# A token embedding whose position table is added by an identity matmul in four of eight groups

## The chip, the core and the metric

The kernel runs on one core of a Trainium2 chip. The metric is the device time of one execution in microseconds (us). Beside the time of each run there is one profiled execution, whose trace gives every instruction's start, duration and what it waited for. All times of the trace count from the start of its span.

## What is computed

Four images of 128 channels and 64 x 64 pixels go through a hybrid block. First the pixels are scored by two depthwise convolutions, and patches of 4 x 4 pixels are ordered by score. Then each pixel becomes a token, and this is the part that the change touches:

```python
pe_re = pe[order]
x_re = jnp.take_along_axis(x_adapted.reshape(B, C, L), order..., axis=2)
x1 = x_re.transpose(0, 2, 1) + pe_re
mu = x1.mean(-1, keepdims=True)
var = ((x1 - mu) ** 2).mean(-1, keepdims=True)
x1n = (x1 - mu) * jax.lax.rsqrt(var + 1e-05) * norm_g + norm_b
```

Behind it come a selective scan over the 4096 tokens, attention with four heads, and a mixture of eight experts. `pe` is the position table, 4096 x 128 float32; adding it and normalising a token do not depend on the order, so the kernel does both before it sorts.

## The kernel before

The program loops over the four images (batches). Each pass is seven stages, each a block in which the five engines run their own instruction lists and meet at the end: `score_and_sort`, `project`, `scan`, `unsort`, `qkv`, `attention`, `ffn`. The change is in `score_and_sort` alone. Nothing reorders the work there: on each engine the instructions run in the order in which the Python code issues them, and semaphores tie the engines together.

The end of `score_and_sort` is the token stage. The 4096 pixels of an image are 32 tiles of 128 tokens, in eight groups g of four tiles (512 columns, `CH`).

- **ScalarE** has earlier copied the pixels into `xp` in patch order (`patches`, L472). In the token stage it has the last Gelu (L495), then a Sigmoid of the head's scores (L498, from PSUM bank 6, waits for semaphore `head`), a Sigmoid of the variance over the channels (L500, waits for `pv`), a square root for the normalisation (L502) and half of the tiles' normalisation (L505).
- **TensorE** runs `token_tiles(g)` (L554 to L563): it transposes the group's four tiles of `xp` into one PSUM bank (`token_bank[g]`, L562) and then adds to semaphore `tr`. It does groups 0 to 5, then the head (`over_channels` with `hwin`, L535, which needs `pv`), then groups 6 and 7, which take the banks of groups 0 and 1 again and so wait until these have been read.
- **VectorE** takes each group in turn (L410 to L422). It adds the bank to the position table `pe_t` and writes the tokens `xt` (L418), then takes `bn_stats` of the four tiles (L422). Before group 2 it computes the variance over the channels (L414 to L416, ends in `pv`). After group 7 follow `bn_aggr` (L425), the final scores (L429 to L434), its half of the normalisation (L440), the rank of each patch and the two slices of the permutation matrix `perm` (L451).
- TensorE transposes each slice of `perm` (L577) and gathers the tokens by matmuls with it (L585); ScalarE takes them out of PSUM (L509), which ends the stage.
- **SyncE** loads the position table by 64 DMAs at the start of the stage (L354, semaphore `pe_in`).

The loop of VectorE before is:

```python
for g in range(NT // 4):
    ...
    dve.wait_ge(tr, g + 1)
    dve.tensor_tensor(xt[...], k.bank(token_bank[g]), pe_t[...], ALU.add).then_inc(k.sem("tokens_embedded"), 1)
    dve.wait_ge(k.sem("tokens_embedded"), g + 1)
    for i in range(4 * g, 4 * g + 4):
        dve.bn_stats(st[:, i, :], xt[:, i * 128:(i + 1) * 128]).then_inc(xt_s, 1)
```

Of the kernel before, what the change touches and what calls it, by code (L numbers as in the profile page):

```python
# [6 lines left out]
ALU, ACT, AX = mybir.AluOpType, mybir.ActivationFunctionType, mybir.AxisListType  # L7
# [3 lines left out]
PS = 4  # L11
NP_ = (H // PS) * (W // PS)
TT = NP_ // 128
# [4 lines left out]
CH = 512  # L18
# [277 lines left out]
def score_and_sort(k, b):  # L296
# [8 lines left out]
    feat, sq, xp = k.at(FEAT_AT, L), k.at(SQ_AT, L), k.at(XP_AT, L)  # L305
# [11 lines left out]
    pe_in, stored = k.sem("pe_in"), k.sem("stored")  # L317
# [7 lines left out]
    xt, pe_t = k.at(XT_AT, L), k.at(PE_AT, L)  # L325
    x1v = k.at(X1_AT, L).rearrange("p (s o) -> p o s", o=OFF)
    tr, xt_s, xtr, std, nrm, pmm = (k.sem(n) for n in ("tr_done", "tokens_stats", "var_ready", "std_ready", "norm_done", "perm_mm"))
# [3 lines left out]
    rs, shift = k.at(LN_AT + 256, NT), k.at(LN_AT + 256 + NT, NT)  # L331
    by_act = [i for i in range(NT) if i % 2]
    token_bank = [4, 5, 0, 1, 2, 3, 4, 5]

    def tap(i, g, j):

        return pad[i][:, RG * g + j // 3:RG * g + j // 3 + RG, j % 3:j % 3 + W]

    def pair(i, g):

        return (NG * i + g) % 3

    def group(t, g):
        return t[:, g * RG * W:(g + 1) * RG * W].rearrange("p (h w) -> p h w", w=W)

    with nc.Block() as block:
# [18 lines left out]
        def _(dve):  # L365
# [44 lines left out]
            for g in range(NT // 4):  # L410
                if g == 2:
                    dve.wait_ge(stored, 32)
                    dve.wait_ge(sums, 2)
                    step(dve.tensor_copy(rows[0], k.bank(6)))  # L414
                    step(dve.scalar_tensor_tensor(rows[1], rows[0], -1.0 / C, rows[0], ALU.mult, ALU.mult))
                    dve.tensor_tensor(rows[1], k.bank(7), rows[1], ALU.add).then_inc(pv, 1)  # L416
                dve.wait_ge(tr, g + 1)
                dve.tensor_tensor(xt[:, g * CH:(g + 1) * CH], k.bank(token_bank[g]), pe_t[:, g * CH:(g + 1) * CH], ALU.add)\  # L418
                    .then_inc(k.sem("tokens_embedded"), 1)
                dve.wait_ge(k.sem("tokens_embedded"), g + 1)  # L420
                for i in range(4 * g, 4 * g + 4):
                    dve.bn_stats(st[:, i, :], xt[:, i * 128:(i + 1) * 128]).then_inc(xt_s, 1)  # L422
            dve.wait_ge(xt_s, NT)
# [32 lines left out]
        def _(act):  # L456
# [36 lines left out]
            for g in range(NG):  # L493
                act.wait_ge(taps_s, (NG + g + 1) * (9 - PT))
                act.activation(group(feat, g), group(feat, g), ACT.Gelu, scale=ca, bias=k.cols[:, C_B2:C_B2 + 1]).then_inc(gelu[1], 1)  # L495
            act.wait_ge(head, 1)
            act.wait_ge(stored, 32)
            act.activation(rows[2], k.bank(6), ACT.Sigmoid, bias=k.cols[:, C_HB:C_HB + 1]).then_inc(sigs, 1)  # L498
            act.wait_ge(pv, 1)
            act.activation(rows[3], rows[1], ACT.Sigmoid, scale=10.0 / (C - 1)).then_inc(sigs, 1)  # L500
            act.wait_ge(xtr, 1)
            act.activation(rs, rs, ACT.Sqrt).then_inc(std, 1)  # L502
            act.wait_ge(shift_s, 1)
# [9 lines left out]
        def _(pe):  # L513
# [40 lines left out]
            def token_tiles(g):  # L554
                if g < 6:
                    pe.wait_ge(taps_s, (2 * NG - 2 + g // 2) * (9 - PT))
                else:
                    pe.wait_ge(k.sem("tokens_embedded"), g - 5)
                pe.wait_ge(k.sem("patches_ready"), g + 1)
                for i in range(4):  # L560
                    at = g * CH + 128 * i
                    last = pe.transpose(k.bank(token_bank[g], 128, 128 * i), xp[:, at:at + 128], k.ident[:, :])  # L562
                last.then_inc(tr, 1)  # L563

            for g in range(6):
                token_tiles(g)
            pe.wait_ge(gelu[1], NG)
            pe.wait_ge(pv, 1)
            over_channels(k.bank(6), k.hwin, lambda n: feat[:, n * CH:(n + 1) * CH]).then_inc(head, 1)
            token_tiles(6)  # L570
            token_tiles(7)
            pe.wait_ge(bd_s, 1)
            pe.matmul(k.bank(3, NP_), k.ones[:, :], bd.rearrange("p n q -> p (n q)"), start=True, stop=True).then_inc(bc, 1)
            for t in range(TT):
                pe.wait_ge(pm, t + 1)
                for u in range(TT):
                    last = pe.transpose(k.bank(7, 128, NP_ * u + 128 * t), k.perm[:, t, 128 * u:128 * u + 128], k.ident[:, :])  # L577
            last.then_inc(pt, 1)
            pe.wait_ge(nrm, NT)
            for o in range(0, OFF, 2):  # L580
                if o == OFF - 2:
                    pe.wait_ge(k.sem("permt_ready"), 1)
                for oo in (o, o + 1):
                    for t in range(TT):
                        last = pe.matmul(k.bank(o // 2, NP_, (oo % 2) * NP_), xt[:, (t * OFF + oo) * 128:(t * OFF + oo + 1) * 128],  # L585
                                         k.perm[:, t, :], start=t == 0, stop=t == TT - 1)
# [1423 lines left out]
def program(nc, ins, out):  # L2010
    with ExitStack() as ctx:
        k = Kernel(nc, ctx, ins, out)
        setup(k)
        with nc.Fori(0, B) as b:
            score_and_sort(k, b)
            project(k)
            scan(k)
            unsort(k, b)
            qkv(k)
            attention(k)  # L2020
            ffn(k, b)
        with nc.Block() as block:
            @block.sync
            def _(sp):
                sp.wait_ge(k.sem("stored"), 32)
# [24 lines left out]
```

## Time and profile before

| | us |
|---|---|
| median of 3 runs | 5550.67 |
| lowest and highest | 5549.47, 5551.52 |
| the profiled execution | 5559.32 |
| its span, first to last instruction | 5557.6 |
| TensorE busy (matmul) | 4773.5 |
| VectorE busy | 4864.6 |
| ScalarE busy | 4017.6 |

The span is the stretch from the first to the last instruction of the profiled execution; its own time is 1.7 us longer, and 8.65 us longer than the median. Every duration of an instruction below is of this one execution. The mean granted clock of TensorE is 0.948 of its full speed. Busy times say how much work an engine has, not who waits for it; for that one reads the timeline of a stage: an idle time behind an instruction stands in square brackets with the engine and line that ended it, and an engine whose rows follow on one another without brackets is the one that the others wait for.

### The profile page before, as it was taken

To read this page: it belongs to the slowest core of one execution; us is meant where nothing else is said; L and a number is where in the kernel's file an instruction comes from. 1 tells how busy PE (TensorE), PEld (TensorE's weight loads), DVE (VectorE), ACT (ScalarE), POOL (GpSimd) and SP (SyncE) were. 2 spreads that over 40 slices of the span, in tenths; PEclk is the share of its full clock that TensorE was granted. 3 is DMA by queue.
4 is the path that set the end of the run, shared out by engine and by line. 5 is a ranking of instruction groups with operands and counts; after the bars stand their busy time and mean duration, and the time that the engine had idled before them with its cause. 6 is when DMAs were issued, how large, how long until landed. Compare 5 with 4: busy or idle time off the path is not lost. (4 is left out here: it accounts for less than half of the span.)

```text
span 5557.6 us, 100602 instructions
## 1 busy us (share of the span) xinstructions
PE 4773.5 (86%) x34168; PEld 1985.8 (36%) x34168; DVE 4864.6 (88%) x6244; ACT 4017.6 (72%) x5832; POOL 1610.2 (29%) x790
## 2 busy tenths in 40 slices
PE   5888879998778887999877887899987788789998
PEld 2333333334333333333433333333343333333334
DVE  6799779998789977999868997799986899689998
ACT  4787569994477757999447784799935778479993
POOL 1388700000048860000004885000000588500000
PEclk9899989999899998999988999899998899999998
DMA  1000030000000003000000000300000000030000
GB/s 41 0 1 0 16 66 10 10 6 24 24 0 1 0 16 66 10 10 6 24 24 0 1 0 16 66 10 10 6 23 24 1 1 0 16 66 10 10 6 31
DMA packets 42112, 89.63 MB, mean 16 GB/s; under 512 B 11595, under 2 KB 27798, under 8 KB 38550
## 3 DMA queue, kind: packets, MB, share of 16 engines
q1 hardware_dynamic: 41622, 83.21, 5.6%
q8 instruction: 294, 4.82, 0.4%
q14 instruction: 196, 1.61, 0.1%
HBM read 28.65 MB, written 8.39 MB: 7 GB/s over the span
## 5 line engine op out<-in xcount | busy, mean ns | idle before, releaser
L1576 ACT ACTIVATE arena<-ps 128x1024 f32<-128x1024 f32 x2048 | 1912.6, 1034 | 190.5 <-PE ps L1539 168.8
L1605 DVE TENSOR_TENSOR arena<-arena 128x1024 f32<-128x1024 f32 x1664 | 1899.6, 1216 | 17.8 <-ACT arena L1576 17.6
L1188 DVE TENSOR_TENSOR_SCAN arena<-ps,hlast,arena 128x512 f32<-128x512 f32 x1024 | 1251.5, 1265 | 28.3 <-ACT hlast L1070 13.9
L1133 POOL TENSOR_TENSOR arena<-arena 128x1024 f32<-128x1024 f32 x512 | 1201.6, 2357 | 240.2 <-ACT arena L1049 173.7
L1539 PE MATMUL ps<-arena 128*32 128x512 f16 x16384 | 1091.0, 382 | 111.2 <-issue 81.0
L1522 PE MATMUL ps<-arena 128*32 128x512 f32 x8192 | 1068.4, 600 | 7.3 <-ACT arena L1576 3.6
L955 PE MATMUL ps<-arena,ident 128*128 128x512 f32 x2048 | 964.8, 595 | 0.0
L1067 ACT ACTIVATE ps<-arena,amat 128x512 f32<-128x512 f32 x1024 | 704.5, 688 | 354.4 <-DVE arena L1188 345.4
L1539 PEld LDWEIGHTS ps<-arena 128*32 128x32 f16 x16384 | 464.6, 97 | 965.9 <-issue 667.8
L1911 POOL MEMSET arena<- 128x1024 f32 x4 | 3.8, 952 | 2452.5 <-POOLq L103 2452.5
L1164 DVE TENSOR_TENSOR arena<-arena,ps 128x1024 f32<-128x1024 f32 x416 | 497.4, 1196 | 80.9 <-PE ps L1024 80.9
L955 PEld LDWEIGHTS ps<-arena,ident 128*128 128x128 f32 x2048 | 392.1, 192 | 354.4 <-issue 326.3
L1522 PEld LDWEIGHTS ps<-arena 128*32 128x32 f32 x8192 | 209.8, 109 | 418.6 <-ACT arena L1576 237.5
L1049 ACT ACTIVATE arena<-ps 128x512 f32<-128x512 f32 x512 | 297.8, 582 | 22.6 <-PE ps L961 22.5
L1024 PE MATMUL ps<-arena,sel 128*128 128x512 bf16 x416 | 164.0, 394 | 138.6 <-DVE arena L1164 125.9
L1989 DVE SCALAR_TENSOR_TENSOR arena<-ps,arena 128x128 f32<-128x128 f32 x1024 | 273.7, 343 | 1.7
L961 PE MATMUL ps<-arena,sel 128*128 128x512 bf16 x512 | 201.1, 393 | 81.0 <-ACT arena L1049 77.7
L1851 PE MATMUL ps<-expw,arena 128*128 128x512 f32 x512 | 252.7, 620 | 11.8 <-DVE arena L1958 8.3
L527 PE MATMUL ps<-arena 128*128 128x512 f32 x512 | 232.4, 615 | 20.0 <-DVE arena L382 20.0
L1122 POOL TENSOR_TENSOR arena<-arena 128x1024 f32<-128x1024 f32 x96 | 226.7, 2361 | 8.6 <-ACT arena L1059 8.6
L643 PE MATMUL ps<-arena,ident 128*128 128x512 f32 x448 | 222.7, 610 | 0.0
L1509 PE MATMUL ps<-arena,ones 128*32 128x512 f32 x1536 | 204.1, 603 | 3.5 <-DVE arena L1605 2.1
(283 smaller groups left out, 4518.4 us busy)
## 6 DMA issues: line engine op xcount, KB each, us to landing
arena<-x SPq DMA_DIRECT2D x36, 512.0 KB, 5.2
arena<-arena SPq DMA_DIRECT2D x64, 256.0 KB, 6.0
arena<-arena SPq DMA_DIRECT2D x64, 224.0 KB, 5.8
arena<-arena SPq DMA_DIRECT2D x28, 512.0 KB, 3.7
arena<-pe SPq DMA_DIRECT2D x256, 32.0 KB, 1.8
out<-arena SPq DMA_DIRECT2D x8, 1024.0 KB, 3.9
expw<-L_ffn_expert_w SPq DMA_DIRECT2D x1, 512.0 KB
wqkv<-L_attn_W_qkv SPq DMA_DIRECT2D x1, 192.0 KB
```

The source lines that it names most:

```text
L955: last = pe.matmul(k.bank(Y_BANK + h), k.ident[:, :], halves(hb[s % RING])[:, h, :], start=False, stop=s == DS - 1)
L1049: act.activation(cs[s % 4], k.bank(C_BANK), ACT.Copy).then_inc(cs_s, 1)
L1067: act.activation(da(s, h), halves(dt[q])[:, h, :], ACT.Exp, scale=k.amat[:, h, s:s + 1]).then_inc(da_s, 1)
L1133: pool.tensor_tensor(halves(hb[s % RING]), halves(hb[s % RING]), cs[s % 4].unsqueeze(1).broadcast_to([128, HD, CH]), ALU.mult).then_inc(hc ...
L1164: dve.tensor_tensor(halves(dbx[(q + owned(s)) % 2]), halves(u[q]), k.bank(B_BANK).unsqueeze(1).broadcast_to([128, HD, CH]), ALU.mult).then ...
L1188: dve.tensor_tensor_scan(halves(hb[s % RING])[:, h, :], da(s, h), halves(injected)[:, h, :], k.hlast[:, s, h, :], ALU.mult, ALU.add).then_ ...
L1522: last = pe.matmul(k.ps[32 * h:32 * h + 32, O * CH:(O + 1) * CH], v[:, j * 128 + 32 * h:j * 128 + 32 * h + 32], probs[(2 * j + h // 2) % 8 ...
L1539: last = pe.matmul(k.ps[32 * t:32 * t + 32, (2 * group[p] + e) * CH:(2 * group[p] + e + 1) * CH], ks[:, h, j * 128 + 32 * t:j * 128 + 32 * ...
L1576: act.activation(probs[p % 8], k.bank(2 * group[p], 2 * CH), ACT.Exp, scale=SCALE / SPLIT ** 2).then_inc(exp_s, 1)
L1605: dve.tensor_tensor(acc[p % 2], acc[p % 2], probs[p % 8], ALU.add).then_inc(acc_s, 1)
L1851: pe.matmul(k.bank(expert_bank(i, hb)), tnt[:, i * 128:(i + 1) * 128], k.expw[:, hb * HE:hb * HE + HE, :].rearrange("p e c -> p (e c)"), s ...
L1989: dve.scalar_tensor_tensor(tile, k.bank(expert_bank(i, hb), C, e * C), gate[:, i, hb * HE + e:hb * HE + e + 1], tile, ALU.mult, ALU.add).t ...
```

## The change

The position table is added on another engine for groups 2, 4, 5 and 7. There TensorE first multiplies the identity with the group's 512 columns of `pe_t` into the bank (`start=True`), and then adds the four tiles of `xp` by ordinary accumulating matmuls against the identity, in place of transposes. ScalarE copies the bank to `xt` and adds to a new semaphore `tokens_copied`; VectorE waits for that and only takes the statistics. The other four groups stay as they were. ScalarE's copies of groups 2, 4 and 5 stand behind the last Gelu and ahead of the two Sigmoids, that of group 7 behind them.

```diff
+    added_by_pe = (2, 4, 5, 7)
+    embedded_v, embedded_a = k.sem("tokens_embedded"), k.sem("tokens_copied")
...
+    def wait_embedded(eng, g):
+        by_act_ = g in added_by_pe
+        eng.wait_ge(embedded_a if by_act_ else embedded_v, sum((o in added_by_pe) == by_act_ for o in range(g + 1)))
...
                 dve.wait_ge(tr, g + 1)
-                dve.tensor_tensor(xt[:, g * CH:(g + 1) * CH], k.bank(token_bank[g]), pe_t[:, g * CH:(g + 1) * CH], ALU.add)\
-                    .then_inc(k.sem("tokens_embedded"), 1)
-                dve.wait_ge(k.sem("tokens_embedded"), g + 1)
+                if g not in added_by_pe:
+                    dve.tensor_tensor(xt[:, g * CH:(g + 1) * CH], k.bank(token_bank[g]), pe_t[:, g * CH:(g + 1) * CH], ALU.add)\
+                        .then_inc(embedded_v, 1)
+                wait_embedded(dve, g)
...
+            def copy_tokens(g):
+                act.wait_ge(tr, g + 1)
+                act.activation(xt[:, g * CH:(g + 1) * CH], k.bank(token_bank[g]), ACT.Copy).then_inc(embedded_a, 1)
+
+            for g in added_by_pe:
+                if g < 6:
+                    copy_tokens(g)
             act.wait_ge(head, 1)
...
+            for g in added_by_pe:
+                if g >= 6:
+                    copy_tokens(g)
             act.wait_ge(xtr, 1)
...
                 else:
-                    pe.wait_ge(k.sem("tokens_embedded"), g - 5)
+                    wait_embedded(pe, g - 6)
                 pe.wait_ge(k.sem("patches_ready"), g + 1)
+                if g == 0:
+                    pe.wait_ge(pe_in, 16 * TT * PS * 8)
+                if g in added_by_pe:
+                    pe.matmul(k.bank(token_bank[g]), k.ident[:, :], pe_t[:, g * CH:(g + 1) * CH], start=True, stop=False)
                 for i in range(4):
                     at = g * CH + 128 * i
-                    last = pe.transpose(k.bank(token_bank[g], 128, 128 * i), xp[:, at:at + 128], k.ident[:, :])
+                    out = k.bank(token_bank[g], 128, 128 * i)
+                    if g in added_by_pe:
+                        last = pe.matmul(out, xp[:, at:at + 128], k.ident[:, :], start=False, stop=i == 3)
+                    else:
+                        last = pe.transpose(out, xp[:, at:at + 128], k.ident[:, :])
                 last.then_inc(tr, 1)
```

TensorE's instructions of the token stage, from group 2 to the last group, are these before (groups 2 to 5, the head, groups 6 and 7; L562 is a transpose of one tile):

```order
L562 MATMUL ps<-ident,arena 128x128 [waits patches_ready,taps_added]
L562 MATMUL ps<-ident,arena 128x128 x3
L535 MATMUL ps<-arena,hwin 32x512 [waits pv_ready,gelu2_done]
L535 MATMUL ps<-arena,hwin 32x512 x7
L562 MATMUL ps<-ident,arena 128x128 [waits patches_ready,tokens_embedded]
L562 MATMUL ps<-ident,arena 128x128 x3
L573 MATMUL ps<-arena,ones 128x256 [waits scores_spread]
```

(The first two rows stand there once for each of the groups 0 to 5, the fifth and sixth for each of the groups 6 and 7.) With the change they are:

```order
L581 MATMUL ps<-arena,ident 128x512 [waits patches_ready,taps_added]
L586 MATMUL ps<-ident,arena 128x128 x4
L588 MATMUL ps<-ident,arena 128x128 [waits patches_ready,taps_added]
L588 MATMUL ps<-ident,arena 128x128 x3
L581 MATMUL ps<-arena,ident 128x512 [waits patches_ready,taps_added]
L586 MATMUL ps<-ident,arena 128x128 x4
L581 MATMUL ps<-arena,ident 128x512 [waits patches_ready,taps_added]
L586 MATMUL ps<-ident,arena 128x128 x4
L553 MATMUL ps<-arena,hwin 32x512 [waits pv_ready,gelu2_done]
L553 MATMUL ps<-arena,hwin 32x512 x7
L588 MATMUL ps<-ident,arena 128x128 [waits patches_ready,tokens_embedded]
L588 MATMUL ps<-ident,arena 128x128 x3
L581 MATMUL ps<-arena,ident 128x512 [waits patches_ready,tokens_embedded]
L586 MATMUL ps<-ident,arena 128x128 x4
```

Three of the four added groups stand in front of the head (L553), one behind it; each has the identity matmul (L581) and four accumulating matmuls (L586) where there were four transposes. A float32 matmul that is no transpose is one row here and two instructions in the trace.

ScalarE's instructions between the last Gelu and the square root are these before:

```order
L495 ACTIVATE arena<-arena,cols,small 128x1024 [waits taps_added] x3
L498 ACT_TABLE_LOAD [waits stored]
L498 ACTIVATE arena<-ps,cols 128x512 [waits head_mm]
L500 ACTIVATE arena<-arena 128x512 [waits pv_ready]
L502 ACT_TABLE_LOAD
L502 ACTIVATE arena<-arena 128x32 [waits var_ready]
```

And with the change:

```order
L503 ACTIVATE arena<-arena,cols,small 128x1024 [waits taps_added] x3
L506 ACTIVATE arena<-ps 128x512 [waits tr_done] x3
L513 ACT_TABLE_LOAD [waits stored]
L513 ACTIVATE arena<-ps,cols 128x512 [waits head_mm]
L515 ACTIVATE arena<-arena 128x512 [waits pv_ready]
L506 ACTIVATE arena<-ps 128x512 [waits tr_done]
L520 ACT_TABLE_LOAD
L520 ACTIVATE arena<-arena 128x32 [waits var_ready]
```

The copies (L506) stand around the two Sigmoids, three ahead and one behind, and both table loads stand behind a copy.

On VectorE the add before the statistics is gone in four groups, whose statistics (now L430) wait for `tokens_copied`.

## Rows read from the trace of the kernel before

**Rows 1.** The page's table of busy time by engine.

```profile
PE 4773.5 (86%) x34168; PEld 1985.8 (36%) x34168; DVE 4864.6 (88%) x6244; ACT 4017.6 (72%) x5832; POOL 1610.2 (29%) x790
```

**Rows 2.** Timeline of VectorE, first batch: start, length, engine, line, operation, [idle before].

```profile
106.48 0.69 DVE L418 TENSOR_TENSOR arena<-ps,arena 128x512 f32<-128x512 f32 x1 [3.01 <-PE ps L562]
107.20 0.87 DVE L422 BATCH_NORM_STATS2 arena<-arena 128x6 f32<-128x128 f32 x4
107.99 0.67 DVE L418 TENSOR_TENSOR arena<-ps,arena 128x512 f32<-128x512 f32 x1
...
109.49 0.67 DVE L414 COPY arena<-ps 128x512 f32<-128x512 f32 x1
...
111.53 0.68 DVE L418 TENSOR_TENSOR arena<-ps,arena 128x512 f32<-128x512 f32 x1
112.25 0.87 DVE L422 BATCH_NORM_STATS2 arena<-arena 128x6 f32<-128x128 f32 x4
...
119.74 0.88 DVE L422 BATCH_NORM_STATS2 arena<-arena 128x6 f32<-128x128 f32 x4
```

**Rows 3.** The same timeline at the end of the stage, VectorE and TensorE.

```profile
133.71 0.35 DVE L451 TENSOR_SCALAR perm<-iota,small 128x256 f32<-128x256 bf16 x1
...
134.12 0.69 PE L577 MATMUL ps<-ident,perm 128*128 128x128 f32 x2 [0.96 <-DVE perm L451]
134.60 15.41 PE L585 MATMUL ps<-perm,arena 128*128 128x256 f32 x64
```

**Rows 4.** Timeline of TensorE in the token stage, first batch.

```profile
105.72 2.84 PE L562 MATMUL ps<-ident,arena 128*128 128x128 f32 x24
111.76 1.92 PE L535 MATMUL ps<-arena,hwin 128*32 128x512 f32 x16 [3.21 <-DVE arena L416]
113.62 1.09 PE L562 MATMUL ps<-ident,arena 128*128 128x128 f32 x8
...
125.78 1.22 PE L573 MATMUL ps<-arena,ones 128*128 128x256 f32 x2 [11.07 <-DVE arena L434]
```

**Rows 5.** Timeline of ScalarE in the token stage, first batch.

```profile
104.76 1.28 ACT L498 ACT_TABLE_LOAD   x1
113.74 0.69 ACT L498 ACTIVATE arena<-ps,cols 128x512 f32<-128x512 f32 x1 [7.70 <-PE ps L535]
...
114.97 1.28 ACT L502 ACT_TABLE_LOAD   x1
```

**Rows 6.** Timeline of TensorE in the convolution: float32 matmuls over 512 columns.

```profile
59.56 28.06 PE L527 MATMUL ps<-arena 128*128 128x512 f32 x65
```

**Rows 7.** Timeline of TensorE in the last stage, first batch: float32 matmuls over 128 columns.

```profile
1305.58 1.91 PE L1826 MATMUL ps<-wout,arena 128*128 128x128 f32 x8
...
1309.97 0.38 PE L1822 MATMUL ps<-outb,ones 128*128 128x512 bf16 x1
1310.19 1.05 PE L1826 MATMUL ps<-wout,arena 128*128 128x128 f32 x8
1311.08 0.38 PE L1822 MATMUL ps<-outb,ones 128*128 128x512 bf16 x1
```

**Rows 8.** Timeline of SyncE's queue: the last loads of the position table.

```profile
59.82 7.36 SPq L354 DMA_DIRECT2D arena<-pe  x16
```

**Rows 9.** ScalarE's copies from PSUM in the next stage: duration min/median/max in ns.

```profile
L778 ACT ACTIVATE arena<-ps x64: 575/598/604, 153.3 to 4324.5; 128x512 f32<-128x512 f32 x64
```

**Rows 10.** Stretches: length, busy PE, PEld, DVE, ACT, POOL, granted clock, DMA share, GB/s.

```profile
1491.50:1494.60 3.10, 0.00 (x0) 0.00 (x0) 3.00 (x9) 0.00 (x0) 0.00 (x0) 1.00 0.00 0
1494.60:1497.10 2.50, 2.42 (x17) 0.58 (x18) 2.43 (x9) 0.00 (x0) 0.00 (x0) 0.78 0.04 7
1497.10:1499.00 1.90, 1.89 (x8) 1.49 (x8) 1.87 (x9) 1.85 (x3) 0.00 (x0) 0.50 0.00 0
1305.50:1307.30 1.80, 1.80 (x10) 1.66 (x9) 0.00 (x0) 0.94 (x1) 0.61 (x1) 0.50 0.40 86
```

**Rows 11.** Timeline of TensorE, second batch: the last eight transposes.

```profile
1497.02 1.97 PE L562 MATMUL ps<-ident,arena 128*128 128x128 f32 x8
```

## The prediction, on record before the changed kernel ran

> **What bounds the kernel now.** I read the page's busy table first. VectorE is busy for 88% of the span and TensorE for 86% [rows 1]; such averages over stages do not say who is waited for in the token stage, so I read that stage by its timeline, in the first of the four batches. The chain of waits is of no use here, since it covers only the last per cent of the span.
>
> VectorE's timeline shows no gap from 106.48 us on [rows 2]. Each of the eight groups costs it an add (L418) and four statistics (L422). From one add to its statistics it is 0.72 us (106.48 to 107.20), from the statistics to the next instruction 0.79 us (107.20 to 107.99), so 1.50 us a group; before group 2 it does the variance over the channels, 2.04 us (109.49 to 111.53). The last statistics start at 119.74. From there VectorE goes on without a gap, through the aggregates and the scores, to the second slice of the permutation at 133.71; 0.4 us later TensorE transposes it (134.12), and the gather matmuls follow at once (134.60) [rows 3]. A microsecond that VectorE saves before 119.74 is therefore a microsecond off the stage, and there are four batches.
>
> TensorE has much slack there [rows 4]: six groups of transposes issued by 108.3, nothing until the head's matmuls at 111.76 (they wait for VectorE's L416), the last two groups from 113.62, and the next matmul of all at 125.78. ScalarE has more [rows 5]: it loads the Sigmoid table at 104.76, waits until 113.74, runs two Sigmoids and loads the Sqrt table at 114.97, which is used only behind VectorE's last statistics.
>
> About 0.2% of this kernel, 11.1 us, is what a measurement can tell from no change; that is 2.8 us a batch.
>
> **The change, part by part.**
> 1. *Four adds leave VectorE* (groups 2, 4, 5, 7): 4 x 0.71 to 0.72 = 2.85 us a batch, 11.4 us in all. This is the ceiling of the gain: nothing else is taken away.
>
> 2. *TensorE gets work.* No row shows an identity matmul in this place, but its two forms stand elsewhere. A float32 matmul over 512 columns is two instructions in the trace; 65 of them take 28.06 us, so 0.86 us for one matmul [rows 6]. Four float32 matmuls over 128 columns are eight instructions; they and one bf16 matmul over 512 columns repeat every 1.11 us (1309.97 to 1311.08), of which the bf16 one takes 0.22 (1309.97 to 1310.19), leaving 0.89 us [rows 7]. An added group is thus 0.86 + 0.89 = 1.75 us. The transposes that it replaces take 0.11 each (24 in 2.84), 0.43 a group [rows 4]. For a bound below, 1.3 us (0.86 for the table and transposes' own price for the rest); above, 0.86 + 4 x 0.43 = 2.6 us, were each small matmul four transposes long. I take 1.75, the row of the same form.
>    The Trainium skill ("TensorE: Matmul & The Clock Gate", Terms) speaks against this edit: transpose mode is four times faster for FP32. By it the added group is the 2.6 us; by the rows the ratio is two (0.22 to 0.11).
>
> 3. *Where that puts TensorE.* From 105.72: groups 0 and 1 0.87, group 2 1.75, group 3 0.43, groups 4 and 5 3.50: issued by 112.27. Only then comes the head, which was ready from 111.7: 1.86 (111.76 to 113.62), so 114.13. Group 6 is issued by 114.56, group 7 by 116.31; with 0.16 for the tail of the last matmul (0.27 long, 0.11 apart), 116.47. The work that is moved in front of the head costs the head 0.5 us, which nobody waits for, as VectorE wants the Sigmoids only behind group 7's statistics. The new wait for the position table at group 0 costs nothing: its loads are issued by 67.2 [rows 8], and VectorE waited for them before, at the same place.
>
> 4. *ScalarE gets four copies* out of PSUM, 0.60 each, by the row of the same shape [rows 9]. From a result of TensorE to its reader I take 0.17 us: group 0's transposes end at about 106.31, the add starts at 106.48. Copies 2 and 4 end near 109.3 and 111.5. Copy 5 starts at 112.60 (112.27 + 0.16 + 0.17), ends at 113.20. The Sigmoid table load now stands behind it: 113.20 to 114.48, and the head's result is there at 114.4, so Sigmoids to about 115.7 (1.23 for both, 113.74 to 114.97 [rows 5]). Copy 7 is ready at 116.64 and finds ScalarE free by 0.9 us; it ends at 117.24. The Sqrt table load then ends at 118.5, while VectorE still aggregates. The order of instructions shows no table load between Gelu and Copy.
>    The Trainium skill ("ScalarE: Activation LUTs", What ACT_TABLE_LOAD costs) puts a load at about 2.7 us with its drain, where this trace has 1.28. By the page ScalarE would be free for copy 7 only at 117.1, the statistics would start at 117.8, and the sum below would be 7.8 us instead of 9.8.
>
> 5. *VectorE waits for copies.* Without waits its statistics would start at 111.53, 113.02, 113.81, 114.60, 116.10 and 116.89 for groups 2 to 7 (112.25 and 1.50 more for each further group, less 0.71 to 0.72 for each add taken out). Copies 2, 4 and 5 are there at 109.3, 111.5 and 113.3, so 1.3 us or more early; group 6's tokens at 114.9, wanted at 115.39. Only group 7 is late: copy 7 ends at 117.24, plus 0.06, so 117.30. VectorE waits 0.41 us, and behind that wait stand the aggregates and all that follows.
>
> 6. *Sum.* 119.74 - 117.30 = 2.44 us a batch, 2.85 less a wait of 0.41; four batches 9.8 us. The profiled execution, 5559.32 us (span 5557.6), would become 5549.5. The median of the runs, 5550.67, lies 8.65 below the profiled one; I take the same 9.8 off it: 5540.9. In the other three batches the same rows stand with the same distances, save that in the second TensorE's clock was at half for the end of the stretch (below); it makes no difference before.
>
> Twenty-four more TensorE instructions a batch, 96 in all, must be fetched; I cost that at nothing beside the 34168 that it has [rows 1].
>
> **The rivals.**
> - *No wait at all.* If the added group costs 1.6 us or less, or results are seen sooner, copy 7 is there by 116.89, and the whole 2.85 comes: 5539.3, 0.205% faster. 0.4 us of TensorE is only 4% of 10.6, which speaks for it; that both prices are of the same form speaks against. The latencies were also taken generously. Chance 0.16.
> - *ScalarE late.* If the load behind copy 5 held it for twice its row, 2.57 us, copy 7 would start at 117.0: 5542.5. The load's row is 1.28 in every place, against it. Chance 0.08.
> - *A small float32 matmul costs four transposes* (the mechanism of the page in part 2). 0.84 more a group, 3.36 in all: group 7's statistics start at 120.66, 0.92 later than before; 5554.3, slower by 0.07%. Rows 7 speak against it directly. Chance 0.06.
> - *TensorE becomes the bound, at half clock* (the rival on the slower side). TensorE may be 2.44 us later than in part 3 before the gain is gone, and 5.2 us before the kernel is slower by over 0.2%. In the second batch the granted clock fell from 1.00 to 0.78 in the head's stretch and to 0.50 behind it, after 3.1 us without a matmul [rows 10]; eight transposes then took 1.97 us instead of 1.09 [rows 11], and eight float32 matmuls at 0.50 1.91 instead of 1.05 [rows 7]. If it is at half from 111.5, the last 4.8 us take 4.8 more, and the statistics start at 122.1: 9.4 us slower in all, 5560; if for the whole stretch, 10.6 more: about 5583. Against it: the pause after which it fell is filled by the change, and until the pause is over the clock stands at 1.00, the higher level of 2.4 GHz [rows 10]. If half clock comes in one batch only, 4.8 of the 9.8 us are lost. Chance 0.05.
> - *Nothing moves*, because what follows is set by something that I don't see (the gather's start, or TensorE's clock at the gather): 5550.7. VectorE's unbroken row of work speaks against it. Chance 0.05.
>
> The forecast has the remaining 0.60, with 5539 to 5544 for itself.
>
> **How the numbers follow.** The range takes the forecast, the first two rivals and a part of the losses in between (one batch at half clock, 5545.7), with a microsecond or two below the ceiling's 5539.3, as much as the runs shown spread (5549.47 to 5551.52): 5537.5 to 5548.0; left out are the last three, 0.16. Faster by over 0.2% (below 5539.6) is the first rival and a little of the forecast's edge: 0.18. Slower by over 0.2% (above 5561.8) is the half clock: 0.05. Within: 0.77.
>
> **What would show it.** In the changed profile: L426 has 16 instructions instead of 32; TensorE's added group is 1.75 us long and its clock 1.00 between 105 and 116; the copies take 0.60; the statistics of group 7 start at 117.3 with an idle of about 0.4 ended by ScalarE, and nothing else on VectorE waits; the gather starts at 132.2. Wrong it is if VectorE also waits at groups 4 to 6, if a wait on TensorE's side is longer than 2.4 us, or if the 2.4 us are there at the aggregates and gone at the gather.

## The result and the profile after

The change makes the kernel slower: 5583.99 us median (5575.99 to 5587.52) against 5551.52 (5549.47 to 5561.6) for the kernel before beside it. The ratio is 1.005, with a 95% interval of 1.0036 to 1.0065. The forecast was a gain of 9.8 us; the medians differ by 32.5 us the other way. The profiled execution of the change took 5577.54 us, its span is 18.2 us longer than that of before, and the granted clock is 0.950 of full speed, where it was 0.948. The two profiled executions stand on opposite sides of their medians (5559.32 us of 5551.52 before, 5577.54 of 5583.99 with the change), so the traces show 18.2 of the 32.5 us.

The profile's page of the change, busy table and instruction fetches (columns of the latter: packets, MB, share of 16 DMA engines):

```profile
span 5575.8 us, 100738 instructions
PE 4786.8 (86%) x34192; PEld 1998.1 (36%) x34264; DVE 4858.9 (87%) x6228; ACT 4028.0 (72%) x5848; POOL 1610.0 (29%) x790
q8 instruction: 302, 4.95, 0.4%
```

And the page of before, its fetches:

```profile
q8 instruction: 294, 4.82, 0.4%
```

Against [rows 1] the instructions are the ones that were announced: 16 fewer on VectorE, 16 more on ScalarE, 96 more weight loads (the matmul column lost some records). No engine's busy time explains 32 us. What the page does show is eight more fetches on q8.

**The token stage did what was forecast.** Timeline of TensorE there, change, first batch (start, length, engine, line, operation, [idle before]):

```profile
107.24 1.02 PE L581 MATMUL ps<-arena,ident 128*128 128x512 f32 x2
108.10 1.05 PE L586 MATMUL ps<-ident,arena 128*128 128x128 f32 x8
108.99 0.60 PE L588 MATMUL ps<-ident,arena 128*128 128x128 f32 x4
...
113.02 1.93 PE L553 MATMUL ps<-arena,hwin 128*32 128x512 f32 x16
```

An added group costs 0.86 + 0.89 = 1.75 us (107.24 to 108.10 to 108.99), the price taken from [rows 6, 7]. VectorE's first add, and ScalarE and VectorE at group 7, same kernel and batch:

```profile
107.07 0.69 DVE L426 TENSOR_TENSOR arena<-ps,arena 128x512 f32<-128x512 f32 x1 [3.01 <-PE ps L588]
...
115.94 0.67 DVE L426 TENSOR_TENSOR arena<-ps,arena 128x512 f32<-128x512 f32 x1
...
116.65 0.87 DVE L430 BATCH_NORM_STATS2 arena<-arena 128x6 f32<-128x128 f32 x4
117.32 0.60 ACT L506 ACTIVATE arena<-ps 128x512 f32<-128x512 f32 x1 [1.07 <-PE ps L586]
117.94 1.28 ACT L520 ACT_TABLE_LOAD   x1
118.02 0.87 DVE L430 BATCH_NORM_STATS2 arena<-arena 128x6 f32<-128x128 f32 x4 [0.50 <-ACT arena L506]
```

VectorE waits once, for 0.50 us (forecast 0.41), ended by the copy, which takes 0.60. This stage starts 0.59 us later than in [rows 2] (107.07 against 106.48), so the last statistics come 10.95 us behind the first add instead of 13.26: 2.31 us a batch where 2.44 was forecast. The other three batches have the same two lengths within 0.02 us. From the last statistics to the gather's first matmul it is 14.86 us in both kernels (119.74 to 134.60 before, 118.02 to 132.88 in the change), so the gain is whole when the gather starts.

**The loss is in the attention.** I cut both traces at the same instructions of each batch (on ScalarE the two square roots of `score_and_sort`, the first and the last copy of the gather and the first and the last exponential, on VectorE the first and the last scan) and added the four batches:

```
stretch                          before    change   difference, us
convolutions and token stage      332.3     321.9     -10.4
normalisation, permutation         59.1      60.0      +0.9
gather                             48.3      49.8      +1.5
projections                       263.0     258.9      -4.1
scan                             1764.7    1760.4      -4.3
unsort and qkv                    449.3     456.6      +7.3
attention                        2093.3    2121.4     +28.1
experts                           507.6     506.8      -0.8
sum                              5517.6    5535.8     +18.2
```

A second profile of the change (the one named "the change again" below) has -7.6, -8.5 and +1.0 in the first, fourth and fifth row, but +7.2 and +29.2 in unsort with qkv and in the attention. So those two are the change's; the rows of a few us in between move from one execution to the next. Where the 7 us of unsort and qkv arise I did not trace.

The stage `attention` is not touched by the change. ScalarE's exponentials bound it. Before, then the change, grouped by line (busy us, mean ns, idle before, by releaser):

```profile
L1576 ACT ACTIVATE arena<-ps 128x1024 f32<-128x1024 f32 x2048 | 1912.6, 1034 | 190.5 <-PE ps L1539 168.8 <-DVE arena L1605 20.3 <-DVE arena L1602 1.1
```

```profile
L1602 ACT ACTIVATE arena<-ps 128x1024 f32<-128x1024 f32 x2048 | 1913.3, 1033 | 217.7 <-PE ps L1565 202.6 <-DVE arena L1631 13.7 <-DVE arena L1628 1.1
```

The same 2048 instructions of the same length wait 27 us longer, and what they wait for more (168.8 to 202.6) is TensorE. There TensorE's list runs over eight chunks of queries: chunk 1 and the last one are written out, and between them `Fori(0, NCH // 2 - 1)` (L1559 before) runs three times over a body of two chunks. Length of a chunk, from its first exponential to that of the next, mean of four batches, in us:

```
chunk                1      2      3      4      5      6
before             63.32  65.10  67.54  65.06  67.42  65.47
change             63.31  65.39  67.67  68.34  67.72  68.32
```

Chunks 3 and 5 are the ones in which the loop branches back, and are 2.4 us longer than their neighbours already before. In the change chunks 4 and 6 lose 2.9 to 3.3 us each as well. TensorE at such a branch, second batch, before:

```profile
2341.11 1.04 PE L1522 MATMUL ps<-arena 128*32 128x512 f32 x8
2344.50 1.05 PE L1539 MATMUL ps<-arena 128*32 128x512 f16 x16 [2.35 <-issue]
2345.37 1.04 PE L1522 MATMUL ps<-arena 128*32 128x512 f32 x8
2346.23 1.88 PE L1539 MATMUL ps<-arena 128*32 128x512 f16 x24
```

and in the change:

```profile
2342.59 1.04 PE L1548 MATMUL ps<-arena 128*32 128x512 f32 x8
2346.14 1.09 PE L1565 MATMUL ps<-arena 128*32 128x512 f16 x16 [2.52 <-issue]
2349.08 1.94 PE L1548 MATMUL ps<-arena 128*32 128x512 f32 x8 [1.84 <-ACT arena L1602]
2350.78 2.79 PE L1565 MATMUL ps<-arena 128*32 128x512 f16 x24
```

ScalarE over the same time, change:

```profile
2346.98 1.94 ACT L1602 ACTIVATE arena<-ps 128x1024 f32<-128x1024 f32 x2 [2.51 <-PE ps L1565]
2352.04 1.02 ACT L1602 ACTIVATE arena<-ps 128x1024 f32<-128x1024 f32 x1 [3.13 <-PE ps L1565]
```

Before there is one hole, 2.35 us ended by "issue", in which TensorE waits for nothing that the profile shows. In the change there is a second one of 1.84 us, some 40 instructions into the body, and behind it the granted clock is down, so that the 24 matmuls take 2.79 us instead of 1.88. The second hole is there at all eight branches back of the change (two in each batch), and at none of before. The profile puts it down to an exponential, which gives these two rows of waits, before and change (us in total, times, longest):

```profile
PE ps L1522 <- ACT arena L1576: 3.6, 4, 0.9
PE ps L1548 <- ACT arena L1602: 20.0, 16, 2.3
```

But the exponential for which this instruction waits had ended by 2344.47 (2346.98 less the idle of 2.51), and TensorE's list has nothing between the end of one group of weight loads at 2346.70 and the next at 2349.07 (PEld are weight loads):

```profile
2346.14 0.56 PEld L1565 LDWEIGHTS ps<-arena 128*32 128x32 f16 x16 [3.42 <-issue]
2349.07 0.20 PEld L1548 LDWEIGHTS ps<-arena 128*32 128x32 f32 x8 [2.38 <-ACT arena L1602]
```

Windows of the change (length, busy PE, PEld, DVE, ACT, POOL, clock, DMA share, GB/s):

```profile
2346.10:2349.10 3.00, 1.12 (x20) 0.37 (x20) 0.00 (x0) 1.94 (x2) 0.00 (x0) 0.65 0.04 11
2349.10:2354.40 5.30, 5.30 (x40) 1.70 (x44) 2.50 (x3) 2.36 (x4) 0.00 (x0) 0.55 0.02 5
```

The instruction fetches of q8, TensorE's by their size and number, in that stretch (start us, duration ns, bytes):

```
before   2341.55 1212 16384    2344.93 1164 16384    2351.68 1395 16384
change   2341.29 1307 16384    2343.11 1347 16384    2346.53  932 16384    2354.11 1080 16384
```

That is the reading which the experiments test. A fetch brings 16384 bytes; I take such a piece as 256 instructions, which runs e2, e5 and e13 below bear out. Once TensorE goes on behind the branch (2344.50, 2346.14) the next piece is asked for 0.4 us later in both kernels. Its transfer takes about a microsecond, and at the second hole TensorE goes on 1.6 us behind the end of that transfer (2346.53 and 0.93 are 2347.46; the next weight load is at 2349.07), so from the asking it is some 2.5 us. Before, no hole follows: enough of the current piece is left to cover that. In the change the body starts, by this reading, some 40 instructions ahead of the end of its piece, TensorE gets there in under 1 us, and stands.

The fetch that the change has more, once at each of the eight branches, is not the one behind the second hole, which before has too (2344.93); it is the one at 2341.29, which starts ahead of the branch (at 2342.05). The change put 48 instructions of TensorE (24 matmuls and 24 weight loads) in front of this loop, and everything behind them lies 48 places further on. The Trainium skill ("Runtime: NRT & Kernel Launch", Instruction fetch mechanics) describes such fetches: instructions come in blocks of 16 KiB, one ahead in sequence, and a taken branch whose target is not in the two blocks at hand stops until it has been fetched. The trace agrees for TensorE, with 16384 bytes a fetch and 2.35 us at the branch before; the 1.84 us more where the piece ends soon behind the branch are this trace's. On the other queue of fetches, q14, on which VectorE's come, a fetch has 8192 bytes here; there the measurement decides.

### The profile page after: what moved, and what is told of

Read it like the earlier page. It is cut to its first block and busy times, and to the rows that moved or that the text cites. A ratio compares the mean times of both kernels' runs of the same rounds, so it can differ in the third digit from the quotient of the medians.

```text
span 5575.8 us, 100738 instructions
## 1 busy us (share of the span) xinstructions
PE 4786.8 (86%) x34192; PEld 1998.1 (36%) x34264; DVE 4858.9 (87%) x6228; ACT 4028.0 (72%) x5848; POOL 1610.0 (29%) x790
## 5 line engine op out<-in xcount | busy, mean ns | idle before, releaser
L1602 ACT ACTIVATE arena<-ps 128x1024 f32<-128x1024 f32 x2048 | 1913.3, 1033 | 217.7 <-PE ps L1565 202.6
L1214 DVE TENSOR_TENSOR_SCAN arena<-ps,hlast,arena 128x512 f32<-128x512 f32 x1024 | 1251.1, 1265 | 29.2 <-ACT hlast L1096 14.7
L987 PE MATMUL ps<-arena,sel 128*128 128x512 bf16 x480 | 187.4, 390 | 95.4 <-ACT arena L1075 91.6
L1050 PE MATMUL ps<-arena,sel 128*128 128x512 bf16 x384 | 150.6, 392 | 120.2 <-DVE arena L1190 116.5
```

Source lines behind the costliest of these rows:

```text
L1214: dve.tensor_tensor_scan(halves(hb[s % RING])[:, h, :], da(s, h), halves(injected)[:, h, :], k.hlast[:, s, h, :], ALU.mult, ALU.add).then_ ...
L1602: act.activation(probs[p % 8], k.bank(2 * group[p], 2 * CH), ACT.Exp, scale=SCALE / SPLIT ** 2).then_inc(exp_s, 1)
```

## The experiments

Theory A: the loss is the displacement of TensorE's instructions, whatever they are. Rival B: it is the new work, through the granted clock, the banks or the semaphores of the token stage. Rival C: it is a displacement, but that of ScalarE's or VectorE's list. VectorE's keeps its length: both traces have 11747 instructions on it, as a wait stands where each add stood. That leaves ScalarE's, four longer. Each of the groups below was measured on one chip with the kernel before beside it. The added instructions are increments of a semaphore that nobody reads.

**e1: displacement without the work.** In the kernel before, 48 increments at the end of TensorE's token stage:

```diff
             token_tiles(7)
+            for _i in range(48):
+                pe.sem_inc(k.sem("pad"), 1)
             pe.wait_ge(bd_s, 1)
```

> The kernel before, with 48 instructions that only add 1 to an unused semaphore on TensorE behind group 7's transposes, where TensorE idles 11 us in each batch. 48 is the number by which the change lengthens TensorE's program per batch (16 transposes of two instructions become 4 times 20). No work is changed. Theory A (the loss is the place of TensorE's attention loop in its program: behind the loop's branch the next piece of instructions must be fetched while the engine is idle): the third and fifth query chunk of attention go from about 65 to 68 us, attention from 524 to 531 us a batch, and the kernel gets slower by 28 us or so, about 5579. Theory B (the matmuls of the change themselves do something to what follows, by the clock or by memory): no change, 5551. Theory C (ScalarE's or VectorE's program is what was moved to a worse place): no change, 5551.

Measured: 5588.50 us against 5555.76, ratio 1.0057 (1.0040 to 1.0074). The attention takes 2118.1 us, unsort and qkv 457.3, as in the change. TensorE at the same branch, second batch:

```profile
2352.34 1.04 PE L1524 MATMUL ps<-arena 128*32 128x512 f32 x8
2355.80 1.05 PE L1541 MATMUL ps<-arena 128*32 128x512 f16 x16 [2.42 <-issue]
2358.70 1.93 PE L1524 MATMUL ps<-arena 128*32 128x512 f32 x8 [1.86 <-ACT arena L1578]
2360.41 2.02 PE L1541 MATMUL ps<-arena 128*32 128x512 f16 x24
```

The second hole is there without a single added matmul, at all eight branches back, and the page's fetches are those of the change:

```profile
q8 instruction: 302, 4.95, 0.4%
```

So TensorE's displacement alone is enough for the whole loss, and a little more (I expected 28 us, and it is 32.7); neither B nor C is needed. Whether B takes part, the next runs show.

**e2: the work without the displacement.** In the change, 206 increments in TensorE's part of the setup, which runs once. With the 48 and two branches they make 256, a whole piece.

```diff
+        @block.tensor
+        def _(pe):
+            for _i in range(206):
+                pe.sem_inc(k.sem("pad"), 1)
```

> The change as it is, with a block ahead of the batch loop in which TensorE executes 206 instructions on an unused semaphore (and two branches) once, while it waits for the weights. With the change's 48 that makes 256 instructions of 64 bytes, 16 KB, the size of one fetched piece, so the attention loop stands again where it stood before within a piece. Theory A: attention back to 523 to 526 us a batch, and the gain of the token stage shows: about 5541 (5538 to 5545). Theory B and C: 5584, as the change.

Measured: 5559.71 against 5555.76, 1.0007 (0.9997 to 1.0017). The attention is at 2096.7 and unsort with qkv at 448.6, so the loss of these stages is gone, as forecast. The time is not: I expected 5538 to 5545. The gain of the token stage does not appear in the median. ScalarE's list is still displaced by its four instructions here.

**e3: ScalarE's own displacement.** In the kernel before, four increments ahead of ScalarE's `wait_ge(xtr, 1)`, as the change puts four instructions there:

```diff
+            for _i in range(4):
+                act.sem_inc(k.sem("pad"), 1)
             act.wait_ge(xtr, 1)
```

> The kernel before with 4 instructions on an unused semaphore on ScalarE ahead of its square root in the token stage, the number by which the change lengthens ScalarE's program. Theory C: slower by some or all of 28 us. Theory A and B: 5551, no change.

Measured: 5565.94 against 5555.76, 1.0016 (1.0007 to 1.0026). Four instructions that do nothing cost 10 us, with 4 to 14 as the interval. That is not C's 28, and the trace does not say where it goes: the attention has 0.9 us more than before, unsort with qkv 1.2, convolutions with token stage 1.2, the projections 3.5, and q8 the same 294 fetches. The projections' row moves by as much between other executions.

**e4: another place.** The change with 46 increments in TensorE's setup (with the branches 48, so 96 in all), and ScalarE's list displaced by four as in the change:

> The change with 46 such instructions (and two branches) ahead of the batch loop on TensorE, so everything there stands 96 instructions later than before inside its 256-instruction pieces. From where the stall lies in the changed trace (some 40 instructions behind the loop's start) the loop's start would stand at about the first instructions of a piece. Theory A: no second fetch soon behind the branch, so attention at most 525 us a batch, and about 5541 or a few us less. Theory B and C: 5584.

Measured: 5572.16, 1.0030 (1.0017 to 1.0043). A miss: I expected the time without loss. The branch back still has no loss behind it (chunk 5 67.81, chunk 6 65.38), but chunk 1 takes 65.2 us instead of 63.3, chunk 4 66.1 instead of 65.1, and unsort with qkv 456.6. The second hole is at none of the eight branches. The place that suits the branch back does not suit the way into the loop and the stages ahead. My rule of the place was too simple.

**e5: both lists put back.** The change with 206 increments on TensorE and 124 on ScalarE (with its four, 128) in the setup:

 Both loops stand in their pieces as before. Theory A, widened by the last runs (the change's work gains 9.8 us, TensorE's shift of 48 costs 33, ScalarE's shift of 4 costs 10): 9 to 10 us faster than before, ratio 0.998. If the token stage's gain were given back by something else that the work does: the same as before.

Measured: 5553.80 against 5555.91, 0.9998 (0.9989 to 1.0007). It is 30 us below the change, but 9 above what I expected, and unsort with qkv is at 453.5 us, between the 449.3 of before and the 456.6 of the change. TensorE has one hole at each of the eight branches again:

```profile
2342.66 1.05 PE L1572 MATMUL ps<-arena 128*32 128x512 f16 x16 [2.05 <-issue]
2343.53 1.04 PE L1555 MATMUL ps<-arena 128*32 128x512 f32 x8
2344.39 1.79 PE L1572 MATMUL ps<-arena 128*32 128x512 f16 x24
```

and the page has one fetch more than before, the setup's piece, and not eight:

```profile
q8 instruction: 295, 4.83, 0.4%
```

**e6 and e7: two more places**, with 158 and with 78 increments on TensorE, ScalarE as in the last:

> As the run with both programs back, but TensorE's stands 208 instructions (or 48 earlier) from its old place within the pieces of 256. Under theory A the place decides by itself: the attention loop starts at about instruction 120 of a piece, its first 136 instructions come with one fetch, so no second stall behind the branch, attention near 523 us a batch or below; other loops and block entries may do better or worse by some us. Expected 5540 to 5556 where before has 5555.

> As the run with both programs back, but TensorE's stands 128 instructions further within the pieces. Theory A: the loop starts at about instruction 40 of a piece, one fetch covers 216 instructions; attention near 523 to 527 us a batch. Expected 5540 to 5565; it maps how the time depends on the place and has no sharper forecast.

Measured: 5555.76, 1.0000 (0.9991 to 1.0009), with the attention at 2091.4; and 5573.93, 1.0036 (1.0023 to 1.0050), with chunk 1 at 67.2 us instead of 63.3 and the attention at 2109.6. The second is a miss: I expected 5540 to 5565. The profile's page of that run has 302 fetches on q8, as many as the change, so their number does not tell the loss. The time is a function of the place, and not of how much is added: against the kernel before 206 cost nothing, 158 nothing, 78 about 18 us, 46 (ScalarE's list not put back) about 16.

**e8: both displacements, no work.** The kernel before with 48 on TensorE and four on ScalarE, at the two places above:

> The kernel before with the change's displacement and without its work: 48 instructions on an unused semaphore on TensorE behind group 7, and 4 on ScalarE ahead of the square root. Theory A: slower than before by 33 + 10 us, ratio 1.008, which is 9 to 10 us more than the change lost (1.005); attention 530 to 532 us a batch and its second chunk 65.4 us. If moving the programs were not the cause, 1.000.

Measured: 5588.90 against 5555.91, 1.0064 (1.0050 to 1.0078). The difference of 33.0 us is that of TensorE's 48 alone (32.7 above). ScalarE's four, worth 10 us by themselves, add nothing here, where I had expected 43 in all. Why is open.

**e9 and e10: no branch.** The attention's loop on TensorE written out, in both kernels:

```diff
-        with pe.Fori(0, NCH // 2 - 1) as cc:
+        for cc in range(NCH // 2 - 1):
```

> The kernel before with TensorE's attention loop (three passes of two query chunks each) written out, so that its program runs straight through attention; ScalarE and VectorE keep their loops. Theory A: a branch back costs a fetch each time, visible as 67.5 instead of 65.1 us in the third and fifth chunk, 2.4 us twice in each of four batches: 19 us faster, ratio 0.9965. If fetching is not what costs, the same as before.

> The change with the same loop written out. Theory A: no branch, so no place in a piece that matters to attention: chunks four and six fall from 68.3 to 65.1 us too, attention near 2073 us in all instead of 2121, and the token stage's 9 us come on top of the gain of the kernel before with the loop written out: 5525 to 5535 where that has 5537 and the change has 5584. Theory B (the work itself slows attention): attention stays about 28 us longer than in the kernel before with the loop written out.

Measured: before 5553.16 against 5554.57, 0.9996 (0.9987 to 1.0005); the change 5552.48, 0.9997 (0.9988 to 1.0006). For the change that is a gain of 31 us: its attention is at 2090.5 us, where the kernel before with the loop written out has 2088.9. So with the loop written out the change's work costs the attention no more than 1.6 us, and B falls. Both times are misses all the same: I expected 0.9965 for before and 5525 to 5535 us for the change. The holes at the branch are gone (chunks 3 and 5 65.2 us), but chunks 4 and 6 are now 67.3 and 66.8. Timeline of VectorE, TensorE and ScalarE in chunk 4, second batch, kernel before with the loop written out:

```profile
2349.90 1.29 DVE L1602 COPY arena<-arena 128x1024 f32<-128x1024 f32 x2 [3.71 <-ACT arena L1576]
...
2355.65 3.35 DVE L1590 RECIPROCAL arena<-ps 128x512 f32<-128x512 f32 x1
...
2359.15 1.06 PE L1509 MATMUL ps<-arena,ones 128*32 128x512 f32 x8 [1.57 <-DVE arena L1590]
...
2361.70 1.03 ACT L1576 ACTIVATE arena<-ps 128x1024 f32<-128x1024 f32 x1 [2.29 <-PE ps L1539]
```

VectorE stood for 3.71 us, takes its reciprocal late, and TensorE and then ScalarE wait for that. The kernel before has the same hole of VectorE, 3.76 us up to 2348.39, beside TensorE's (and 3.1 to 3.9 us at all eight branches); that TensorE's had hidden it is argued. VectorE has a loop of its own there, and the trace of this run places the hole at its branch back: the branch (L1612) is issued at 2344.8, two fetches of 8192 bytes start on q14 at 2345.8 and 2348.2, and nothing of VectorE starts from 2346.2 to 2349.9 but one instruction of its sequencer between the two. I did not write that loop out.

**e11: the change again**, beside these two:

> The change once more, on the chip of the other runs of this call: 1.005 to 1.0055 times the kernel before, as measured, and less by 1.5 thousandths than the kernel before with its programs displaced alone (1.0064), the difference being the gain of the work.

Measured: 5583.66 against 5554.57, 1.0054 (1.0040 to 1.0067), as expected, and on another chip than the first measurement.

**e12 and e13: what the work is worth at a harmless place.** The kernel before with 254 and 128 increments in the setup (TensorE's and ScalarE's whole pieces), and once more the change with both lists put back:

> The kernel before with whole pieces of added instructions ahead of the batch loop: 254 and two branches on TensorE (256), 128 on ScalarE. It is the control for the change with both programs back, whose padding reaches the same places: if the padding is free and only the place within a piece counts, 1.000 times the kernel before; if padding ahead of the loop costs by itself what is missing there (7 us of the token stage's 9), 1.0013.

> The change with both programs back once more, now beside its control on the same chip. If the work's gain arrives whole, 9 us under the control (ratios apart by 0.0017); if a part is given back behind the token stage (the gather's matmuls with TensorE's clock rising later, some 2 us, and more that is not found), 2 to 7 us under it.

Measured: 5559.95 against 5558.31, 1.0003 (0.9994 to 1.0012), and 5553.59, 0.9994 (0.9985 to 1.0003). Both have every later instruction at the place within its piece where the kernel before has it, and the attention takes 2090.5 us in both. So the work of the change is worth 5559.95 - 5553.59 = 6.4 us at the median; for the pair with the loop written out it is 5553.16 - 5552.48 = 0.7. The intervals of such a difference are some 5 us to either side, so neither is told from nothing, and the first not from the whole 9.2 us. The traces of e12 and e13 show what is gained and given back: convolutions and token stage 322.1 against 332.4 us and projections 261.9 against 266.6, but normalisation with permutation 60.6 against 59.2, gather 51.0 against 48.3, scan 1766.6 against 1764.7, unsort with qkv 454.3 against 450.5. The projections' difference is within what executions of one kernel differ by (258.9 and 254.5 us in the change). From the first square root on, the two traces differ by 5.3 us.

What is lost at the gather is the clock's. The gather's matmuls, before, in the change, and in the change with both lists put back (e13; e12 has 61.5 us, as before):

```profile
L585 PE MATMUL ps<-perm,arena 128*128 128x256 f32 x256 | 61.4, 404 | 0.0
```

```profile
L611 PE MATMUL ps<-perm,arena 128*128 128x256 f32 x256 | 63.7, 415 | 0.0
```

```profile
L618 PE MATMUL ps<-perm,arena 128*128 128x256 f32 x256 | 65.5, 424 | 0.0
```

They start at the lower granted level, 0.50 (1.2 GHz), in all of them. From the gather's start to the rise it is 2.4 to 3.2 us before, 2.3 to 5.3 in the change and 4.4 to 5.1 in e13 (the kernel before has single batches above 5 too, in e8 and e9). That gives back 2.3 of the 9 us in the change and 4.0 in e13, which is the whole of the two rows normalisation with permutation and gather there (1.4 and 2.7).

## Why the prediction was wrong

**Right, with their sizes:** the ceiling of part 1 (2.31 gained and 0.50 waited are 2.81 of 2.85), the price of an added group in part 2 (1.75 us), the copies and table loads of part 4 (0.60 and 1.28 us), the single wait of part 5 (0.50 for 0.41), and the gain at the last statistics in part 6 (2.31 for 2.44 us a batch). Clock 1.00 through the stretch rules out the rival of half clock. These two windows of the first batch show it, and over 12 us from the first add to the last statistics it is 1.00 in each of the four batches of the change:

```profile
105.70:108.60 2.90, 2.90 (x23) 1.81 (x16) 1.49 (x6) 0.00 (x0) 0.00 (x0) 1.00 0.00 0
114.80:117.30 2.50, 2.49 (x18) 1.74 (x14) 2.47 (x12) 1.44 (x3) 0.00 (x0) 1.00 0.00 0
```

The rival by which a small float32 matmul costs four transposes also fell: four took 0.89 us where a group of transposes takes 0.43, two to one, as the rows said. Of ScalarE late and of no wait at all nothing came. Of the signs of being wrong, a gain that is there at the aggregates and gone at the gather did not come either: it is lost behind the gather's start.

**The step that failed** is the sentence behind the sum: "Twenty-four more TensorE instructions a batch, 96 in all, must be fetched; I cost that at nothing beside the 34168 that it has." The number of fetches is not what costs (e7 has as many as the change and loses about half as much). What costs is that the instructions behind them move: 33 us when 48 that do nothing are put in (e1, e8), about nothing when the change's own 48 are filled up to a whole piece (e5, e13). The count was wrong too: each of the 24 matmuls brings a weight load, so the list is 48 longer in each pass, 96 being only the matmuls of four batches. The busy times and counts of [rows 1] were the wrong place to look. The trace of before had the clue, the holes "<-issue" at each branch back, 2.35 us in the one shown, and the 16384-byte fetches beside it, in a stage that I did not read because the change did not touch it.

**The assumption behind it** was that a gain or loss stays in the stage that is edited. Here 9 us were gained in the edited stage, as forecast, and some 35 lost three and more stages later. The rival on the slower side in the prediction, half clock, named the wrong mechanism. The time that it gave, about 5583, is near the measured one by chance.

**What also fell:** that a microsecond off the last statistics is a microsecond off the end. It was one up to the gather's start. Behind that, with the displacement undone, the medians of the two pairs show 0.7 and 6.4 us of the 9, each with some 5 to either side. In the traces 2 to 4 us go at the gather, by the clock; where the others go is not settled.

**No version beats the kernel before** by what can be told: the best are the change with both lists put back (0.9994, 0.9998) and the one with the loop written out (0.9997), all with intervals across 1.

## What to carry to other kernels

Where an engine's list has a loop as long as this one (some 3400 instructions of TensorE, 13 pieces), any instruction added or removed ahead of it moves the loop's start within a fetched piece, and in this kernel that cost more than the edit was worth. Before believing or blaming a change of a few tenths of a per cent, put the same number of empty instructions into the old kernel, and fill the new one up to a whole piece, for each engine whose list got longer; the two runs separate place from work. In the traces, look for idle time ended by "issue", or by an engine that had long been done, just behind a loop's branch.

## What was not expected of the hardware

- A branch back over TensorE's long body cost 2.05 to 2.52 us without a matmul in the stretches shown, and the start's place within a piece a further 1.8 us some 40 instructions later.
- 48 empty TensorE instructions cost 33 us of 5556, four empty ScalarE ones 10 (4 to 14), and both together 33.
- Taking away the holes at TensorE's branch brought 1.4 us of 5555, within the interval. VectorE's of 3.71 us stood beside them; that one had hidden the other is the reading, and no run shows it by itself.
- A fetch of 16384 bytes took 0.9 to 1.4 us in the stretches shown, and TensorE went on 1.6 us behind the end of the one for which it stood.
- The gather's matmuls found the clock at 0.50 in both kernels. In e13 the rise came some 2 us later than in e12 in each batch, which cost 4.0 of the 9 us; what sets the moment of the rise no run here shows.
